# Attention probabilities' tiles 2 and 3: six chunks by squares and memory, two by transposes, and a new order at the start

## What is computed

```python
q, k_new, v_new = h @ wq.T, h @ wk.T, h @ wv.T         # h = layernorm(x)
k = concatenate([ctx, k_new]);  v = concatenate([ctx, v_new])
attn = softmax(q @ k.T * scale)                        # 512 rows, 1024 keys
x = x + tanh(g_xattn) * ((attn @ v) @ wo.T)
hidden = relu((layernorm(x) @ sign(up).T) * up_scale)
x = x + tanh(g_ffn) * ((hidden @ sign(down).T) * down_scale * output_scale)
```

## Time and profile before

| | us |
|---|---|
| median of 3 runs (lowest, highest) | 578.24 (578.15, 578.38) |
| the profiled execution | 578.1 |
| its span, first to last instruction | 576.3 |
| TensorE busy | 571.3 |
| VectorE busy | 398.1 |
| ScalarE busy | 280.8 |

### The profile page before, as it was taken

The page is one execution under the profiler, slowest core; times in us unless marked ns, Lnnn a source line. Parts: engine busy times, 40 slices in busy tenths (PEclk is TensorE's granted clock), DMA queues, the critical chain, the costliest instruction groups (busy, mean ns, idle before and its releaser), DMA issues.

```text
span 576.3 us, 6967 instructions
## 1 busy us (share of the span) xinstructions
PE 571.3 (99%) x2640; PEld 476.2 (83%) x2640; DVE 398.1 (69%) x560; ACT 280.8 (49%) x401; POOL 123.1 (21%) x109
## 2 busy tenths in 40 slices
PE   8999999999999999999999999999999999999997
PEld 7988888888888888888888888888888888888886
DVE  5889546688685588682588686777569545766655
ACT  4884512564321564321565454756468355555531
POOL 5006312102034002033012043332322022422000
PEclk9999999999999999999999999999999999999999
DMA  8712762124424155425114833373811311230011
GB/s 300 243 61 40 181 182 74 52 58 114 106 72 75 44 176 155 101 74 74 68 43 107 257 111 109 99 158 111 210 46 36 147 37 38 108 112 36 5 70 73
DMA packets 93392, 59.97 MB, mean 104 GB/s; under 512 B 71856, under 2 KB 76208, under 8 KB 92976
## 3 DMA queue, kind: packets, MB, share of 16 engines
q1 hardware_dynamic: 93360, 59.54, 35.8%
HBM read 44.84 MB, written 14.69 MB: 103 GB/s over the span
## 4 chain that ended last, share of the span: by engine, by line
PE 98%; DVE 1%; DMA 0%; issue 0%
PE proj L674 28%; PE score L790 19%; PE turn L775 13%; PE score L708 9%; PE turn L674 8%; PE score L674 8%; PE proj L775 5%; PE proj L708 4%; PE score L916 2%; PE turn L666 1%; PE score L666 1%; PE turn L989 1%; PE score L989 0%; DMA rows<-in_x 0%; DVE stats L1622 0%; PE score L923 0%
## 5 line engine op out<-in xcount | busy, mean ns | idle before, releaser
L790 PE MATMUL score<-down_signs,hid_split 128*128 128x512 f32 x480 | 128.4, 391 | 0.0
L790 PEld LDWEIGHTS score<-down_signs,hid_split 128*128 128x128 f32 x480 | 89.2, 188 | 18.3 <-DVE hid_split L1675 0.5
L674 PE MATMUL proj<-four_x,weights 128*128 128x512 f32 x336 | 76.8, 390 | 0.0
L674 PEld LDWEIGHTS proj<-four_x,weights 128*128 128x128 f32 x336 | 63.1, 188 | 13.0
L606 POOL TENSOR_TENSOR four_x<-raw_ctx,four_x 128x2048 fp32r<-128x2048 f32 x7 | 32.6, 4655 | 132.7 <-ACT four_x L1020 132.7
L1675 DVE TENSOR_TENSOR hid_split<-hid,hid_split 128x512 fp32r<-128x512 f32 x64 | 44.4, 696 | 16.0 <-ACT hid_split L1236 15.8
L775 PE MATMUL turn<-ops_b,up_ops 128*128 128x512 f32 x192 | 51.3, 390 | 0.0
L1236 ACT ACTIVATE hid_split<-hid 128x512 fp32r<-128x512 f32 x64 | 40.0, 630 | 21.4 <-PE turn L989 13.7
L1227 ACT ACTIVATE hid<-hid,hid_gain 128x512 f32<-128x512 f32 x48 | 34.7, 724 | 22.7 <-DVE hid L1704 11.1
L674 PE MATMUL score<-weights,four_x 128*128 128x512 f32 x192 | 45.3, 390 | 0.0
L674 PE MATMUL proj<-weights,four_x 128*128 128x512 f32 x192 | 45.3, 392 | 0.0
(11 more groups left out here) (144 smaller groups left out, 946.4 us busy)
## 6 DMA issues: line engine op xcount, KB each, us to landing
raw_w<-in_ffn_w SPq DMA_DIRECT2D x21, 512.0 KB, 3.3
raw_ctx<-in_ctx_turned SPq DMA_DIRECT2D x4, 1024.0 KB, 5.9
raw_ctx<-in_ctx SPq DMA_DIRECT2D x4, 1024.0 KB, 5.7
probs_rows<-probs_squares SPq DMA_DIRECT2D x64, 64.0 KB, 1.9
squares_placed<-probs_rows SPq DMA_DIRECT2D x8, 512.0 KB, 4.3
raw_x<-block_rows SPq DMA_DIRECT2D x4, 1024.0 KB, 7.3
result<-rows SPq DMA_DIRECT2D x15, 256.0 KB, 2.0
rows<-in_x SPq DMA_DIRECT2D x3, 1024.0 KB, 9.2
```

The source lines that it names most:

```text
L674: last = pe.matmul(bank, lhs(l), rhs(r), start=start and i == 0, stop=stop and i == 2)
L790: last = pe.matmul(wide(r), hid_split[:, n % HR, s, r * P:(r + 1) * P], down_signs[:, chunk_of(q), :], start=(q == 0 and s == HI), stop=(q ...
```

## The change

`FAR` says how many of the 8 key chunks of a row tile take the way by squares: 6 for row tiles 2 and 3, 4 for 0 and 1 as before. So `turn_probs` has two transposes for tiles 2 and 3 and four for 0 and 1, and the copies out follow (`turned_cols`). `probs_squares` moves from under `probsT` to under the queries, has 768 columns, and waits for A22's product; ScalarE's copy of the first half no longer waits for the second half's stores. SyncE stores tiles 2, 3 and 0, loads the first half, stores tile 1 and loads the second. `turn_probs` moves to behind the first two terms of V's tile 2. The new-key products begin with chunks 2 and 3, then wait for the first half of the squares and take 0 and 1.

At the start the key weights lie by quarters in memory (`wk[e]`), ScalarE rounds the second quarter ahead of the turned rows, `keep_busy(6)` goes, the first high x high pass of e = 0 and 1 goes row tile by row tile with matmuls of 128 columns (`first_k_tile`), and VectorE takes the third tile's statistics ahead of the turned rows. Left out below: the same rules in the helpers of TensorE, ScalarE and VectorE that copy turned tiles, and the `stop` flags of the later half passes.

```diff
--- before.py
+++ after.py
@@ -160,17 +160,19 @@
         late_squares = normed
+        FAR = {2: RT + 2, 3: RT + 2, 0: RT, 1: RT}
+        FAR_ALL = RT + 2
         PAIRS = ((2, 3), (0, 1))
-        probs_squares = at("probs_squares", 160, [P, RT, ROWS])
+        probs_squares = at("probs_squares", 112, [P, RT, FAR_ALL * P])
         squares_placed = at("squares_placed", 176, [P, KC, ROWS])
-        probs_rows = nc.dram_tensor("probs_rows", (BATCH, ROWS, ROWS), F32).ap()
+        probs_rows = nc.dram_tensor("probs_rows", (BATCH, FAR_ALL * P, ROWS), F32).ap()
         probs_rows_v = probs_rows.rearrange("b (c p) q -> b p c q", p=P)
         probs_squares_v = probs_rows.rearrange("b (j n) (t i a) -> b t i n j a", n=SQ, i=P // SQ, a=SQ)
         def placed_part(h):
             first = PAIRS[h][0] * P
-            return slice(None), slice(0, RT), slice(first, first + 2 * P)
+            return slice(None), slice(0, FAR[PAIRS[h][0]]), slice(first, first + 2 * P)
         def scaled(c, r):
@@ -230,6 +232,9 @@
                 return proj[:, n - 2, :] if n >= 2 else turn[:, n, :]
             return turn[:, n % 4, :] if n % 4 < 2 else score[1][:, n % 4 - 2, :]
+
+        def turned_cols(n):
+            return 4 * P if n < RT else KEYS - FAR[TILE_ORDER[n % RT]] * P
         def proj_bank(n):
             if n < DC:
@@ -427,7 +432,7 @@
                 for r in half:
                     sp.dma_start(rows[:, r, :], x_v[0, :, r, :]).then_inc(x0_in[r], 16)
                 for e in half:
-                    sp.dma_start(raw_of[W_K][:, e, :], wk[:, e].rearrange("p c n -> p (c n)")).then_inc(wk_in[e], 16)
+                    sp.dma_start(raw_of[W_K][:, e, :], wk[e].rearrange("p c n -> p (c n)")).then_inc(wk_in[e], 16)
             sp.dma_start(raw_of[W_Q], wq.rearrange("p e c n -> p e (c n)")).then_inc(w_in[W_Q], 16)
             sp.dma_start(raw_ctx[:, :, :], ctx_turned_v[0]).then_inc(ctx_in, 16)
             sp.dma_start(raw_of[W_V], wv.rearrange(row_tiles, p=P)).then_inc(w_in[W_V], 16)
@@ -452,18 +457,27 @@
             def place_squares(b):
-                for h, pair in enumerate(PAIRS):
-                    for t in pair:
-                        sp.wait_ge(probs_squared, tile_done(b, t))
-                        for i in range(P // SQ):
-                            sp.dma_start(probs_squares_v[b, t, i], probs_squares[i * SQ:(i + 1) * SQ, t].rearrange(
-                                "n (j a) -> n j a", a=SQ)).then_inc(squares_stored[h], 16)
+                def store_tile(t):
+                    sp.wait_ge(probs_squared, tile_done(b, t))
+                    far = FAR[t] * P // SQ
+                    for i in range(P // SQ):
+                        sp.dma_start(probs_squares_v[b, t, i][:, 0:far],
+                                     probs_squares[i * SQ:(i + 1) * SQ, t, 0:far * SQ].rearrange("n (j a) -> n j a", a=SQ)
+                                     ).then_inc(squares_stored[t not in PAIRS[0]], 16)
+
+                def place(h):
+                    sp.wait_ge(squares_stored[h], 2 * STORED * (b + 1))
+                    first, last = PAIRS[h]
+                    sp.dma_start(squares_placed[placed_part(h)],
+                                 probs_rows_v[b][:, 0:FAR[first], first * P:(last + 1) * P]).then_inc(placed[h], 16)
+
+                for t in TILE_ORDER[:3]:
+                    store_tile(t)
                 sp.wait_ge(scored, product_scored(b, A22, 1))
-                for h, pair in enumerate(PAIRS):
-                    sp.wait_ge(squares_stored[h], 2 * STORED * (b + 1))
-                    cols = slice(pair[0] * P, (pair[1] + 1) * P)
-                    sp.dma_start(squares_placed[placed_part(h)], probs_rows_v[b][:, :, cols]).then_inc(placed[h], 16)
+                place(0)
+                store_tile(TILE_ORDER[3])
+                place(1)
             def block_rows_back(b):
                 sp.wait_ge(squares_out[b], STORED)
...
@@ -748,7 +762,7 @@
             def turn_probs(b, i):
                 t = TILE_ORDER[i]
                 pe.wait_ge(exp_done, tile_done(b, t))
-                turn_job(turn0(b) + i, cols(probs[:, t, ROWS:KEYS]))
+                turn_job(turn0(b) + i, cols(probs[:, t, FAR[t] * P:KEYS]))
             def v_jobs(b):
@@ -761,11 +775,11 @@
                         pe.wait_ge(proj_lo, values_out(b, r - 2))
                     for i, (lhs, rhs) in enumerate(v_terms(r)):
                         last = product(proj_bank(proj0(b) + r), lhs, rhs, i == 0, i == DC - 1)
+                        if r == 2 and i == 1:
+                            pe.wait_ge(score_sums, 10 * (b + 1))
+                            for k in range(RT):
+                                turn_probs(b, k)
                     last.then_inc(proj_done, 1)
-                    if r == 1:
-                        pe.wait_ge(score_sums, 10 * (b + 1))
-                        for i in range(RT):
-                            turn_probs(b, i)
             def up_product(g, k, bank, left, i, start, stop):
@@ -855,14 +869,20 @@
                 n = proj0(b)
                 pe.wait_ge(turn_lo, turn0(b) + RT)
+
+
+                pe.wait_ge(proj_lo, values_out(b, 2))
+                for e in (0, 2, 3):
+                    product(proj_bank(n + DC + e), *new_terms(e)[2], True, False)
+                pe.wait_ge(proj_lo, values_out(b, 3))
+                for e in (0, 2, 3):
+                    product(proj_bank(n + DC + e), *new_terms(e)[3], False, False)
+                for i in (2, 3):
+                    product(proj_bank(n + DC + 1), *new_terms(1)[i], i == 2, False)
+                pe.wait_ge(placed_lo, 2 * b + 1)
                 for e in range(DC):
-                    if e == 1:
-                        pe.wait_ge(proj_lo, values_out(b, 3))
-                    for i, (lhs, rhs) in enumerate(new_terms(e)):
-                        if e == 0:
-
-                            pe.wait_ge(proj_lo, values_out(b, max(i, 2)))
-                        last = product(proj_bank(n + DC + e), lhs, rhs, i == 0, False)
+                    for i in (0, 1):
+                        last = product(proj_bank(n + DC + e), *new_terms(e)[i], False, False)
                 if last_batch:
                     last.then_inc(new_read, 1)
                 pe.wait_ge(placed_lo, 2 * b + 2)
@@ -908,13 +928,20 @@
                 pe.wait_ge(normed_done, r + 1)
                 turn_job(r, cols(first_normed[:, r, :]))
-            def first_k_half(e, half, one_pass):
+            def first_k_tile(e, r):
+
+                cut = slice(r * P, (r + 1) * P)
+                for c in range(DC):
+                    pe.matmul(proj_bank(e)[:, cut], weights[:, W_K, HI, e, c * P:(c + 1) * P], xT[:, HI, c, cut],
+                              start=r == 0 and c == 0, stop=False)
+
+            def first_k_half(e, half, one_pass, ends=False):
                 i, (l, r) = one_pass
                 cut = slice(half * 2 * P, (half + 1) * 2 * P)
                 for c in range(DC):
                     last = pe.matmul(proj_bank(e)[:, cut], weights[:, W_K, l, e, c * P:(c + 1) * P], xT[:, r, c, cut],
-                                     start=i == 0 and c == 0, stop=i == 2 and c == DC - 1)
+                                     start=i == 0 and c == 0, stop=ends and c == DC - 1)
                 return last
             def keep_busy(n):
@@ -929,17 +956,19 @@
             turn_first(0)
             keep_busy(3)
             turn_first(1)
-            keep_busy(6)
-            pe.wait_ge(turn_hi, 2)
-            for e in (0, 1):
-                pe.wait_ge(w_hi, e + 1)
-                first_k_half(e, 0, PASS[0])
+
+            for r in (0, 1):
+                pe.wait_ge(turn_hi, r + 1)
+                for e in (0, 1):
+                    pe.wait_ge(w_hi, e + 1)
+                    first_k_tile(e, r)
+            pe.wait_ge(w_ready[W_K], 1)
+            first_k_half(0, 0, PASS[2])
             pe.wait_ge(turn_lo, 2)
-            for e in (0, 1):
-                first_k_half(e, 0, PASS[1])
-            for e in (0, 1):
-                pe.wait_ge(w_ready[W_K], e + 1)
-                first_k_half(e, 0, PASS[2])
+            first_k_half(0, 0, PASS[1], True)
+            first_k_half(1, 0, PASS[1])
+            pe.wait_ge(w_ready[W_K], 2)
+            first_k_half(1, 0, PASS[2], True)
             pe.wait_ge(w_hi, 3)
             first_k_half(2, 0, PASS[0])
             first_k_half(2, 0, PASS[1])
...
@@ -1103,14 +1132,11 @@
             def probs_out(b, i):
                 t = TILE_ORDER[i]
-                turn_out(turn0(b) + i, probsT[:, HI, RT:KC, t * P:(t + 1) * P])
+                turn_out(turn0(b) + i, probsT[:, HI, FAR[t]:KC, t * P:(t + 1) * P])
             def placed_out(b, h):
                 act.wait_ge(placed[h], 16 * (b + 1))
                 part = placed_part(h)
-                if h == 0:
-
-                    act.wait_ge(squares_stored[1], 2 * STORED * (b + 1))
```

(30 more changed lines are left out.)

## The result

| | before | after |
|---|---|---|
| median, us | 578.38 (578.15 to 578.82, 5 runs) | 584.57 (583.81 to 585.22, 5 runs) |
| ratio, 95% interval | | 1.0107 (1.0096 to 1.0119) |
| span of the profiled execution, us | 576.3 | 583.3 |
| TensorE busy, us | 571.3 | 572.3 |

The change makes the kernel 6.2 us slower, 1.1%. The direction was forecast, the size was not: 581.6 was predicted, with a range up to 583.6.

What follows compares the result with a forecast made beforehand. TensorE, busy 99% of the span, was taken as the bound. Per batch 1.23 us of wait and restart less 0.44 saved gave +3.2 over four; with +0.3 at the start, 581.6 us, range 579.1 to 583.6.

Steps and rivals of the forecast that it cites:

- The wait in V (parts 2 and 3): Before V's tile 2, TensorE waits for VectorE's copy of tile 0: 0.55 uncovered plus 0.52 from wider squares, each batch.
- The wide square transposes: On VectorE, squares of row tiles 2 and 3 grow from 512 to 768 columns: 0.26 us more each.
- The restart: TensorE resuming after waiting for V's copy: exposed weight load of the first matmul, 0.11 us, ends 0 and 0.2.
- The removed transposes: On TensorE, 4 of 16 transposes go in each batch, saving 0.44 us, 1.75 over four batches.
- The round trip (part 4): Squares through memory for the new-key products: ready at 327.7 in batch 3, 0.5 us before wanted, costing nothing.
- Rival A: Squares return from memory late, a second TensorE wait: 1.0 us in batch 3, 583.6 in all; chance 0.20.
- What stands behind the round trip on SyncE: Row facts, sign and row loads issued after the second load leave 2.5 us later: nothing, up to 0.5 for all batches.
- The start (part 5): Key weights by quarters and first key matmuls of 128 columns: +0.3 us, ends -0.7 and +0.8.
- The gain of an earlier beginning: At the start, TensorE's first key matmul goes at 8.0, not 8.36: 0.36 us gained, ends 0 and 0.7.
- the split of matmuls: At the start, 8 matmuls of 256 columns become 16 of 128: 0.79 us more, lower end 0.

Runs made afterwards that it cites:

- the move alone: Kernel before with only the sixteen transposes of probabilities moved behind the first two terms of V's tile 2: 581.92 us against 578.29, ratio 1.0061.
- the second run above: Changed kernel with the transposes of probabilities put back behind V's tile 1, ahead of the wait for tile 0's bank: 581.84 us, ratio 1.0057.
- the split one: Changed kernel with transposes split around V's tile 2, V's tile 0 copied first, batch 0 in SyncE's old order with four chunks: 580.99 us, ratio 1.0039.

## Why the prediction was right and wrong

- **The wait in V (parts 2 and 3): right in place, cause and size.** 1.07 and 0.05 were worked out, 1.15 was measured, and the move alone, 0.55 + 0.05, was confirmed by its own kernel. The wide square transposes were put at 0.26 more each; they take 0.97 instead of 0.70.
- **The restart: mis-sized.** 0.11 was taken, with 0.2 as the upper end; it is 0.29 (1.65 us for six matmuls of 0.227). Four times 0.18 is 0.7 us of the miss. By itself it would have left the time inside the range.
- **The removed transposes: right as a term** (0.44), but the second run above shows that at the old place the wide squares would have eaten it through the last exponential. The prediction saw that exponential only behind the new place, where it has slack.
- **The round trip (part 4): right.** It was to be no wait, with a cover of 0.5. The chunks that need it come at 334.37 in batch 3 (the chain's 333.01 and six matmuls) and the squares are ready at 331.70 + 1.76 = 333.46: a cover of 0.9, the thinnest of batches 1 to 3. Rival A did not happen in the changed kernel and did in the split one.
- **What stands behind the round trip on SyncE: the step that failed.** "What SyncE issues behind it ... leaves 2.5 us later; I put that at nothing, with up to 0.5 for all batches." In batch 0 it left 5.9 us later, the row facts' own DMA took 3.0 us longer, and the term that was put at nothing cost 2.5 us. Three things were missed. The second load was put 5.2 us behind the first (324.6 against 319.4 in batch 3), and came 7.6 behind it there and 8.2 in batch 0, because tile 1's stores, issued behind the first load, took 4.4 to 4.9 and 5.1 to 6.0 us where stores with no load ahead took 1.9. The facts' DMA was not given a longer time at all. And nobody was asked who waits for the facts: VectorE, whose start was free to slip 4.5 us against TensorE for the first wait and some 3.7 for the second, slipped 6.3 (7.5 less TensorE's own 1.2). What made the DMA itself longer stays open. In the profiles the forecast was +3.5 and the result +7.0; of the difference 2.5 is this step, 0.7 the restart, and the rest 0.1 each at the start and in the wait in V. The median exceeds the forecast by 3.0.
- **The start (part 5): nothing instead of +0.3**, inside its bounds. The changed kernel's own profile has the first key matmul at 8.06 and W_Q's products at 21.42, near the 8.0 and 21.3 that were forecast, but other profiles of the same start have 20.88 to 21.42, so that agreement is in part luck. The gain of an earlier beginning was put at 0.36 and was 0.30 there and 0.83 in the kernel with the start alone; the split of matmuls was put at 0.79 and cost 0.98. The two cancel within what varies.

The sum, with what was measured: 0.4 at the start of this profile, 4 x 1.0, 2.5, in all 7.0 of span.

## What to carry to other kernels

Before moving work past a wait, look at what that work was covering: here sixteen transposes hid a copy that came 0.6 us late, and the chain before showed no gap for exactly that reason. Where an engine works in a fixed order, a DMA moved ahead of others changes the time of all that follow; follow each of them to its reader, small ones above all. Ask for each reader how much delay is free, and add up the later issue and the longer transfer before comparing. And when one wait is removed, work out when the engine will reach the next one, and whether the new order makes that one's data later: 1.4 us of the cover of the round trip was the wait itself.

## What the runs showed of the hardware

- A DMA of 4 KB in pieces of 4 bytes (the row facts) was on its way 12.1 to 15.1 us in batch 0 of the eleven kernels. The same DMA comes twice more in each; the third, issued near 200 us when no squares are on their way, took 16.7 to 18.6 us. In the run with the facts moved ahead a load of 768 KB issued 0.5 us before it took 9.9 us instead of 5.7. What it spends this time on is open: in that kernel the profile's DMA column was 1.45 at 12 GB/s from 66 to 68 us and 0.93 at 10 GB/s from 68 to 70, while in the changed kernel it was 0.00 from 76 to 84.2, the facts still under way.
- Stores issued behind a load landed after it, and took longer for it: with no load ahead 1.7 to 1.9 us for 64 KB in batch 0 of the kernel before, 3.6 to 4.0 behind a load of 512 KB, and stores of 64 KB behind one of 768 KB 5.1 to 6.0 in batch 0 and 3.2 to 4.9 in the other batches. It is no rule that all DMAs of a queue land in order: with the facts moved ahead, issued at 59.80 and landed at 73.0, the first store behind them, issued at 60.36, landed at 71.3. The Trainium skill (DMA: Bandwidth & Descriptors, Queues, rings and completion order) has each engine take descriptors in ring order and says that a later DMA may still complete first; the two cases agree with the two halves of this.
- Issuing a store of 768 pieces of 128 bytes took SyncE 0.57 us as a rule, one of 512 pieces 0.50: not in proportion (0.75). Single issues took 1.1 to 2.3.
- Matmuls of 128 columns with a new 128x128 weight each cost 0.119 to 0.121 us, as much as those of 256 columns. The Trainium skill (TensorE: Matmul & The Clock Gate, Back-to-back issue gap) gives 0.081 for 128; the measurement, with float32 operands, differs and decides here.
- After the wait in V, the first six matmuls of 512 columns took 0.29 to 0.32 us more than their steady pace, in every profile with that wait; after the waits of the split run, twelve took 0.30 to 0.34 more.
